# Four transformer layers on one core: reordered queues in layers 0, 2 and 3

## The reference

```python
x = x + L0_xattn(layernorm(x), ctx)   # 16 heads of 8, q and k scaled to length 1, own layernorm of the output
x = x + L0_ffn(layernorm(x))          # 8 experts of 256 hidden, gates of the 2 largest of a softmax
x = x + L1_xattn(layernorm(x), ctx)   # ternary weights, int8 activations
x = x + L1_ffn(layernorm(x))          # an expert for each eighth of a micro batch
x = x + L2_xattn(layernorm(x), ctx)   # 8 heads of 64, softmax, projection
x = x + L2_ffn(layernorm(x))          # below
x = x + L3_xattn(layernorm(x), ctx)   # 16 heads of 64, softmax, projection
x = x + L3_ffn(layernorm(x))          # 2 of 8 experts per batch, chosen by the scores of its token 0
```

## Time and profile before

| | us |
|---|---|
| runs shown | 1435.8, 1440.9, 1441.27 |
| median of them | 1440.9 |
| the profiled execution | 1438.69 |
| its span, first to last instruction | 1436.4 |
| TensorE busy | 1365.3 |
| VectorE, ScalarE, GpSimd busy | 1004.6, 941.8, 745.3 |

### The profile page before, as it was taken

One profiled execution on the slowest core, in us unless ns is written; L12 is line 12 of the kernel. 1 busy time (PEld: TensorE's weight loads), 2 busy tenths in 40 slices (PEclk: granted clock), 3 DMA queues, 4 the chain that ended last, 5 costly groups with the idle time before them and its releaser, 6 DMA issues. The chain is left out here.

```text
span 1436.4 us, 30044 instructions
## 1 busy us (share of the span) xinstructions
PE 1365.3 (95%) x9799; PEld 1013.6 (71%) x9799; DVE 1004.6 (70%) x2375; ACT 941.8 (66%) x1951; POOL 745.3 (52%) x763
## 2 busy tenths in 40 slices
PE   7999989998998989999999999999999999999988
PEld 5555558897664867777775777677777777777767
DVE  6877856778667667777776566577767767777683
ACT  4787776785667547676664465576766667676654
POOL 5455641111762236666665486465656656565542
PEclk9999999999999999999999999899999999999999
DMA  6300000000001300000001000000000000000003
GB/s 174 83 0 0 1 8 23 1 1 1 1 1 48 89 0 1 2 0 0 0 0 38 1 0 2 0 1 1 1 0 0 0 0 0 0 0 0 1 3 87
DMA packets 31516, 20.55 MB, mean 14 GB/s; under 512 B 9569, under 2 KB 29000, under 8 KB 31432
## 3 DMA queue, kind: packets, MB, share of 16 engines
q1 hardware_dynamic: 31204, 19.38, 4.9%
q10 hardware_dynamic: 228, 0.10, 0.0%
HBM read 18.42 MB, written 1.05 MB: 14 GB/s over the span
## 5 line engine op out<-in xcount | busy, mean ns | idle before, releaser
L2368 POOL TENSOR_TENSOR arena<-arena,l3a_rinv 128x512 f32<-128x512 f32 x256 | 260.3, 1040 | 200.5 <-DVE l3a_rinv L2767 200.1
L2662 ACT ACTIVATE arena<-l3a_scores_ps,l3a_nmax 128x512 f32<-128x512 f32 x256 | 174.8, 685 | 125.2 <-DVE l3a_nmax L2761 125.0
L2368 POOL TENSOR_TENSOR arena<-arena,l2a_rinv 128x512 f32<-128x512 f32 x128 | 129.9, 1039 | 91.0 <-DVE l2a_rinv L2767 90.8
L2761 DVE TENSOR_REDUCE l3a_nmax<-l3a_scores_ps 128x2 f32<-128x1024 f32 x128 | 155.8, 1218 | 20.3 <-PE l3a_scores_ps L2441 20.3
L874 ACT ACTIVATE l0a_prob<-l0a_scores_ps,l0a_k_scale 128x1024 f32<-128x1024 f32 x128 | 135.5, 1112 | 34.6 <-PE l0a_scores_ps L724 33.9
L2472 PE MATMUL l3a_work_ps<-l3a_probT,l3a_v 128*64 128x256 f32 x1024 | 124.6, 385 | 3.1 <-DVE l3a_probT L2773 3.1
L2662 ACT ACTIVATE arena<-l2a_scores_ps,l2a_nmax 128x512 f32<-128x512 f32 x128 | 87.4, 686 | 60.2 <-DVE l2a_nmax L2761 60.1
L2773 DVE COPY l3a_probT<-l3a_scores_ps 128x512 f32<-128x512 f32 x65 | 44.9, 691 | 96.1 <-PE l3a_scores_ps L2449 96.0
L2472 PEld LDWEIGHTS l3a_work_ps<-l3a_probT,l3a_v 128*64 128x64 f32 x1024 | 67.8, 136 | 52.1 <-issue 19.5
L2761 DVE TENSOR_REDUCE l2a_nmax<-l2a_scores_ps 128x2 f32<-128x1024 f32 x64 | 77.7, 1217 | 9.5 <-PE l2a_scores_ps L2441 9.5
L738 PE MATMUL l0a_pv_ps<-l0a_prob,l0a_v 128*32 128x256 f32 x1024 | 70.2, 392 | 0.0
(11 more groups left out here) (778 smaller groups left out, 3823.6 us busy)
## 6 DMA issues: line engine op xcount, KB each, us to landing
l1f_w<-in_L_ffn_w SPq DMA_DIRECT2D x16, 256.0 KB, 2.8
arena<-in_ctx SPq DMA_DIRECT2D x4, 384.0 KB, 5.4
w_l_w<-in_L_ffn_W SPq DMA_DIRECT2D x1, 1024.0 KB
arena<-in_L_ffn_W SPq DMA_DIRECT2D x16, 64.0 KB, 1.9
out_x<-x_tokens SPq DMA_DIRECT2D x8, 128.0 KB, 1.9
x_tokens<-in_x SPq DMA_DIRECT2D x1, 896.0 KB, 7.4
const<-in_constants SPq DMA_DIRECT2D x1, 525.0 KB
w_l_wo<-in_L_xattn_Wo SPq DMA_DIRECT2D x1, 512.0 KB
```

What stands on the lines that cost most here:

```text
L2368: e.tensor_tensor(prob[n][:, :], prob[n][:, :], bcast(rinv[:, n:n + 1], [P, S]), ALU.mult).then_inc(m.prob_ready, 1)
L2662: e.activation(prob[at][:, :], scores_bank(b, c, u), ACT.Exp, bias=nmax[:, at:at + 1], accum_out=rsum[:, at:at + 1]).then_inc(m.exp_ready, 1)
L2761: e.tensor_reduce(nmax[:, at:at + 2], sps[:, first:first + 1024].rearrange("p (h k) -> p h k", h=2), AX.X, ALU.max, negate=True).then_inc( ...
```

## The change

Only orders change, with one operation that goes from VectorE to GpSimd. In layer 0 attention group 1's `keep_pv` comes right behind the first `divide`, `norm_y` behind `clamp_k`, `k_low` before `square_k`, and eps is added by GpSimd from a constant tile. In layer 0 FFN `keep_gates` comes before `gelus`. In the layer 2 experts the low parts of the K side go to steps 2 and 7, the power and shifts to step 5, the scaling to steps 6 and 7 in halves, and TensorE waits for the Q and K sides apart. In the wide attentions the norm tiles are turned in `tps[0]`. The operations of `Choice` stand at other places among the last batch's.

```diff
@@ apply_scalar(self, e, n, x, tiles=None)
-        for i in range(self.tiles):
+        for i in tiles or range(self.tiles):
@@ l0_attention, gpsimd
+            e.memset(eps[:, :], EPS).then_inc(m.filled, 1)
+            e.wait_ge(m.filled, 5)
...
             def finish(b):
+                e.wait_ge(m.y_stats, 2 * TPB * b + 2 * TPB)
+                e.tensor_tensor(yvar[:, :], mv[:, :, 1], eps[:, :], ALU.add).then_inc(m.yvar_ready, 1)
                 e.wait_ge(m.yvar_ready, b + 1)
...
                     q_norms(b + 1)
+                    k_low(b + 1)
                     square_k(b + 1)
-                    k_low(b + 1)
@@ l0_attention, vector: y_statistics and turn
-                e.wait_ge(m.y_stats, 2 * TPB * b + 2 * TPB)
-                e.tensor_scalar(yvar[:, :], mv[:, :, 1], EPS, None, ALU.add).then_inc(m.yvar_ready, 1)
...
                     if n == 7:
                         divide(b, 0, 0)
+                        keep_pv(b, 1)
                         if after:
                             split_q(b + 1)
-                        if before:
-                            norm_y(b - 1)
-                    if n == 8:
-                        keep_pv(b, 1)
                     if n == 9 and after:
                         keep_kS(b + 1, 0, 0)
                         clamp_k(b + 1)
+                    if n == 9 and before:
+                        norm_y(b - 1)
@@ l0_ffn, scalar
+                if x == 7 and more:
+                    keep_gates(c + 1)
                 if n + 2 < SLOTS:
                     gelus(n + 2)
...
-                if x == 7 and more:
-                    keep_gates(c + 1)
@@ wide_attention, tensor
             def turn_finished(b, n):
-                e.wait_ge(m.k_lo_ready, n + 3)
+                e.wait_ge(m.q_lo_ready, n + 3)
                 if isinstance(b, int) and b < 0:
-                    late.tensor(e, 0, tps[1])
+                    late.tensor(e, 0, tps[0])
                 else:
-                    ahead.tensor(e, b, tps[1])
+                    ahead.tensor(e, b, tps[0])
...
-                        project_q(*on)
                         if c == 3 and not first:
                             e.wait_ge(ahead.z_kept, b)
                         if not (c == 3 and first):
-                            project_k(*on)
+                            project_q(*on)
+                        project_k(*on)
                     closing = c == C - 1 and not more
-                    if closing:
+                    if closing and experts:
                         join_last(0, range(0, C - 3))
                     turned_in_cycle(b, c, turn_c, more, 0)
                     turned_in_cycle(b, c, turn_c, more, 1)
...
+                    if closing and not experts:
+                        join_last(0, range(0, C - 3))
...
                     if c == 3 and first:
                         e.wait_ge(late.z_lo_ready, 1)
-                        project_k(*on)
+                        project_q(*on)
@@ wide_attention, vector
+                    if choosing and c == 5:
+                        experts.early.vector_pick(e, 0)
+                        experts.early.vector_without_largest(e)
+                        experts.early.vector_second(e)
+                    if choosing and c == 6:
+                        experts.early.vector_pick(e, 1)
+                        experts.early.vector_one_hots(e)
                     if c >= 2 or not first:
                         keep_o(*back)
                     if choosing and c == 4:
                         experts.early.vector_take(e, tps[0])
+                        experts.early.vector_largest(e)
                     if not joins:
                         invert(b, c, 0)
-                    if choosing and c == 5:
-                        experts.early.vector_pick(e, 0)
-                        experts.early.vector_without_largest(e)
-                    if choosing and c == 6:
-                        experts.early.vector_pick(e, 1)
-                        experts.early.vector_one_hots(e)
                     if turns_here:
                         keep_turned(*turn_c, 0, turned_bank(b, c, 0))
                     invert(b, c, 1)
-                    if choosing and c == 4:
-                        experts.early.vector_largest(e)
-                    if choosing and c == 5:
-                        experts.early.vector_second(e)
@@ l2_ffn experts, gpsimd
-                        if n == 1:
+                        if n == 2:
                             low_part(u, 1, c_lo, cum, c_hi)
                         if n == 4 and u + 1 < TURNS:
                             low_part(u + 1, 0, q_lo, qT, q_hi)
-                        if n == 5 and u + 1 < TURNS:
-                            low_part(u + 1, 0, c_lo, cum, c_hi)
-                        if n == 6 and u > 0:
+                        if n == 5 and u > 0:
                             ahead.gpsimd(e, u - 1)
                             ahead.shifts(e, u - 1)
+                        if n == 7 and u + 1 < TURNS:
+                            low_part(u + 1, 0, c_lo, cum, c_hi)
                         product_low(STEPS * u + n)
@@ l2_ffn experts, tensor: products
                     if u == 0 and n == 0:
-                        e.wait_ge(m.first_lo_ready, 1)
+                        e.wait_ge(m.hi_ready, 1)
                     elif c == 0:
-                        e.wait_ge(m.lo_ready, 4 * u + 2 * r)
+                        e.wait_ge(m.lo_ready, 4 * u + 2 * r - 1)
...
                     if u == 0 and n == 0:
                         e.wait_ge(m.first_lo_ready, 2)
+                    elif c == 0:
+                        e.wait_ge(m.lo_ready, 4 * u + 2 * r)
@@ l2_ffn experts, scalar
-                        if n == 7 and before:
-                            ahead.apply_scalar(e, u - 1, tiles_of(u - 1))
+                        if n in (6, 7) and before:
+                            ahead.apply_scalar(e, u - 1, tiles_of(u - 1), range(2 * (n - 6), 2 * (n - 6) + 2))
```

More of the change, by code:

```diff
@@ L281, in shifts, with apply_scalar @@
         e.tensor_tensor(self.shift[:, :], self.neg_mean[:, :], self.rstd[:, :], ALU.mult).then_inc(self.shift_ready, 1)
-    def apply_scalar(self, e, n, x):
+    def apply_scalar(self, e, n, x, tiles=None):
         e.wait_ge(self.shift_ready, n + 1)
-        for i in range(self.tiles):
+        for i in tiles or range(self.tiles):
             e.activation(self.z[i], x[i], ACT.Identity, scale=self.rstd[:, i:i + 1],
@@ L360, in l0_attention @@
         own_slot = s.sb("own_slot", [P, 2])
+        eps = s.sb("eps", [P, TPB])
         zT = s.sb("zT", [P, T])
@@ L2315, in late_rows @@
         def late_rows():
-            rows = tps[1][:, 0:len(last_tiles) * P]
+            rows = tps[0][:, 0:len(last_tiles) * P]
             width = last_tokens(g.z_hi).shape
@@ L2491, in join_last @@
                     e.wait_ge(m.q_lo_ready, C * B)
-                    e.wait_ge(m.x_updated, TPB * (B - 1))
+                    e.wait_ge(ahead.z_kept, B - 1)
                 if i == 1 and pairs.start == 0:
                     e.wait_ge(m.k_lo_ready, C * B)
-                    e.wait_ge(ahead.z_kept, B - 1)
                     if experts:
@@ L2548, in turn @@
                         else:
-                            e.wait_ge(m.k_lo_ready, C * B)
-                            ahead.tensor(e, b - 1, tps[1])
+                            e.wait_ge(m.q_lo_ready, C * B)
+                            ahead.tensor(e, b - 1, tps[0])
                     if choosing and c == 4:
@@ L2710, in turn @@
                     if c == 3 and not first:
-                        keep_z(b - 1, tps[1])
+                        keep_z(b - 1, tps[0])
                     exps(b, c, 2)
@@ L2716, in turn @@
                     if onward:
-                        keep_q(*on[0:2])
                         if not (c == 3 and first):
-                            keep_k(*on[0:2])
+                            keep_q(*on[0:2])
+                        keep_k(*on[0:2])
                     keep_turned(*turn_c, 1, turned_bank(b, c, 1))
@@ L3621, in products @@
                     for k, (x, y) in enumerate(((v_hi, q_hi), (v_lo, q_hi), (v_hi, q_lo))):
+                        if u == 0 and n == 0 and k == 2:
+                            e.wait_ge(m.first_lo_ready, 1)
                         last = e.matmul(xps[n % 2][:, :], x[r][:, pair], y[r][:, :], start=k == 0, stop=k == 2)
```

## The result

| kernel | median us | runs | ratio to before, 95% interval |
|---|---|---|---|
| before | 1441.09 | 4 (1435.8 to 1441.96) | |
| changed | 1419.6 | 4 (1419.24 to 1421.64) | 0.9885 (0.986 to 0.9911) |
| changed, timed again | 1419.61 | 4 (1418.24 to 1420.32) | 0.9888 (0.9873 to 0.9904) |

By the ratios the change makes the kernel 1.1% faster. The medians of the table differ by 21.5 us; in the second set of runs, where the kernel before had a median of 1435.32, they differ by 15.7. The kernel before scatters more (1435.8 to 1441.96 in the first set, 1431.63 to 1439.24 in the second) than the changed one. The forecast was 1423. The two profiled executions, 1438.69 and 1421.64, differ by 17.05; the sum of the prediction (-15.9) is to be held against that.

A forecast was written before the change was run, and what follows sets the result against it. TensorE, busy for 95% of the span, was taken as the bound. The terms -9.5 - 3.9 + 1.4 + 1.7 - 5.6 = -15.9 us, against the profiled 1438.7, gave 1422.8, forecast as 1423; the 8-in-10 range was 1413 to 1432.

The forecast's parts named there:

- Layer 0 attention, forecast -9.5: Layer 0 attention: TensorE's eight waits for l0a_pv and a clock drop go, less new waits: -9.5 us, bounds -5 and -11.5.
- new wait of 0.3 us in each of seven turns: Layer 0 attention: TensorE would newly wait for VectorE's later work, up to 0.3 us a turn, 2.0 us in all.
- rival (b): Layer 0 attention: TensorE meets kS and qS 1 us sooner, half the gain comes back; 1431 with clock drops, chance 0.22.
- The lock: VectorE operations reading and writing SBUF end only when GpSimd's running one does; L1063 takes 1280 ns against 171.
- Rival (c): Layer 0 attention: VectorE holds GpSimd, which bounds the turn; no gain at 3.8 us late, 1451 at 5.5; chance 0.03.
- Gates, forecast -3.9: Layer 0 FFN: TensorE's idle of 2.55 us and its clock drop of 1.5 go, 0.2 lost: -3.9 us.
- Experts, forecast +1.4: Layer 2 experts: new waits for c_lo cost +4.0 us, the last turn gives -2.3, the start -0.3: +1.4.
- forecast 0.3: Start of layer 2 experts: first products no longer wait for the low parts, nothing to -0.4 us, taken as -0.3.
- Norm tiles, forecast +1.7: Wide attentions: queries wait for the z copy, +3.2 us, less 1.5 for late tiles: +1.7, bounds -5.0 and +3.5.
- +0.25 a batch: Wide attentions: queries start 0.25 us later in each of 13 batches, waiting for ScalarE's copy of z: +3.2 us.
- -1.5 for the late tiles: Wide attentions: TensorE's waits of 0.8 and 0.7 us for k_lo at the late tiles go: -1.5 us.
- Choice, forecast -5.6: Last batch of layer 3: waits of 3.1 and 0.8 us and a clock drop of 1.7 go: -5.6, bounds -3.5 and -6.

The follow-up runs named there:

- keep_pv run: The kernel before with only keep_pv(b, 1) moved behind the first divide: 1434.61 us, ratio 0.9984 (0.9963 to 1.0006).
- both together: The changed kernel with eps back on VectorE and square_k before k_low again: 1429.92 us, ratio 0.9956.
- each alone: Two runs of the changed kernel: with eps back on VectorE, 1420.14 us; with square_k before k_low again, 1419.14 us.

## Why the prediction was right, and which terms were off

The mechanisms were right for the most part, but that the total came within 1.2 us of the traces' difference is partly luck. Layer 0 attention gave 3.7 us more than forecast and the choice 1.1 more; the norm tiles cost 2.7 more, and stretches of low clock that belong to none of the edits took about 1.

**Layer 0 attention, forecast -9.5, measured -13.2.** The mechanism held: keep_pv was late behind work that GpSimd's operations stretched, and it now stands 2.5 us ahead of need (forecast 2.8). The term mis-sized is the new wait of 0.3 us in each of seven turns, 2.0 in sum. None came but in the first full turn, where L672 waits 1.30 for kS, as before L676 waited 1.27 for pv. Instead turns 1 to 5 gained 1.65 each and not 1.15. Of that 1.22 is the wait at L676, 0.30 the second wait behind it (for kS, at L667), and 0.27 falls at L658, where `divide` no longer stands behind the stretched addition (its rows above); 0.14 is given back. In the last turn the wait of 1.88 and its clock are gone, but a new one of 0.51 for the exponentials takes part of it. I had not looked at what L667 waits for, though rows 0.5 us apart would have shown it. The keep_pv run shows why that matters: without norm_y moved behind keep_kS, and with both stretched operations as they were, the gain is none. It was the forecast's rival (b) in its pure form, and the other edits of this stage keep it away. What norm_y's place alone is worth was not tried.

**The lock.** L994 is at 0.69 in all turns and the small additions at 0.2, as forecast. That these shortenings are needed is shown only for both together (10.3 us); each alone moves the median by 0.5 one way or the other. The prediction's rule, that a VectorE operation which reads and writes SBUF ends only when GpSimd's running one does, is too wide. In the kernel before the two statistics L1057 on y run from 103.22 to 103.71, inside k_low, and are over 1.6 us before it.

**Rival (c).** VectorE does hold GpSimd: keep_residual (L505) takes 1.04 beside VectorE's two-input L1021, 0.61 before (its line was L502). The Trainium skill ("SBUF — State Buffer", section "SBUF: two separate sides") has a VectorE operation with two SBUF inputs as a holder of that lock against GpSimd; the trace agrees with these two numbers. But k_scales has slack, and no exponential waits for the scales. The direction was right and the size, 0.43 a turn, far from the 3.8 at which it would have decided.

**Gates, forecast -3.9, measured -3.8.** Of the idle 2.55 and the clock, as worked out. The run with gates and choice undone shows both parts again, the clock's at twice the length.

**Experts, forecast +1.4, measured +1.2.** The three waits for c_lo were forecast at 1.6, 1.2 and 1.2, and are 1.62, 1.45 and 1.45 (4.5 in all). At the end L292 waits 0.22 instead of 2.02 and the clock stays full, less a wait of 0.68 for the last prod_lo. From the first K-side product to the last update the shift adds 1.2 us; the other 1.3 of the table's +2.6 arose before them, where low clock lasts longer in the changed kernel's trace. The start gave nothing of the forecast 0.3: the first product waits 0.96 instead of 1.68, and the next ones lose that again. Taking c_lo two steps later was a loss of 5 us hidden in a gain.

**Norm tiles, forecast +1.7, measured +4.4.** Two terms are wrong, the +0.25 a batch and the -1.5 for the late tiles. The six batches of layer 2 took the shift from -17.4 to -14.8, and seven of layer 3 from -12.4 to -10.0, so 0.43 and 0.34. The waits of 0.70 and 0.78 for the late tiles are gone, but L2451, a few products on, now waits 0.27 and 0.37 for the copy L2781, and each late tile gave only 0.3 by the shift: a wait handed on once more. I counted from the start of the queries to the end of the copy, 0.19 in layer 3 and 0.20 in layer 2, and 0.06 for the hand-over. By the rows it is 0.13 from the copy's end to L2402 (593.97 to 594.10), and behind an idle the first of the products lasts 0.38 instead of 0.28; with these two the sum is 0.42 a batch.

**Choice, forecast -5.6, measured -6.7.** All operations stand at 0.13 to 0.22, and all four waits are gone, with 1.5 of clock. The wait of 0.33 at L2449 and the slower first products behind each wait had been left out of the sum. The clock's part is not the edit's to promise. The prediction puts the stretch at 1396 right behind the idle of 2.1, but that idle ended at 1390.83, and only the wait of 0.85 at 1395.56 stands just ahead of it; in the run with the choice undone the same waits brought no low clock at all.

**The rest** is +0.9 at the start, -1.4 at the start of layer 2 attention, +1.3 ahead of the experts and +0.3 in between, about +1 in sum. The second and third are stretches of low clock: at the start of layer 2 attention 0.50 and 0.70 from 516 to 524 before, 0.57 from 500 to 504 and then 1.00 after; ahead of the experts 0.61 from 806 to 810 before, 0.78 and 0.50 from 788 to 796 after. Why is not explained here, and it differs from one execution to the next: in the second trace of the changed kernel the low clock at the start of layer 0 FFN (0.57 from 196 to 200 in the first) is missing, which alone is worth 1.3. So a gain that lies in the clock is not sure from one pair of traces.

## What to carry to other kernels

A wait named in the list hides the next one on the same engine: before an early copy is priced, look at what the instruction right behind the waiting one needs, and move that as well, or the wait is only handed on. In a kernel that is bound by one engine, price each moved producer against the time that its consumer wants it, step by step; here the low part c_lo and the queries of cycle 3 were worse off than before, and moving c_lo and the copy of z one place forward gave 12.7 us more, against 15.7 for the whole change on the same chip. When two edits guard against one thing, undo them together, or each looks idle.

## What the hardware showed that was not expected

- The length of a pause does not settle whether TensorE's clock falls. It stayed at 1.00 behind waits of 1.62 and 1.45 us in the experts (changed kernel), and fell to 0.57 behind 1.40 in three turns of layer 0 attention (keep_pv alone) but not in the four turns before them. In the last batch of layer 3 it fell after waits of 1.01, 2.09, 0.33 and 0.85 in the kernel before, and stayed at 1.00 after 1.01, 2.11, 0.33 and 0.85 with the choice undone. What tells these apart was not tried.
- VectorE and GpSimd hold each other in both directions: 1.27 instead of 0.17 for an addition of 128x2 on VectorE, and 1.04 instead of 0.61 for a multiplication of 128x256 on GpSimd.
